# Scaling and masking half of the attention scores on ScalarE instead of VectorE, in the steps of a perceiver layer that have no value product

## The reference

```python
B, L, D = 32, 64, 128; S = 1601; HEADS, HEAD_DIM = 16, 64
q = layernorm(x) @ Wq                         # 32 x 64 tokens, 16 heads
k = ctx @ Wk; v = ctx @ Wv                    # 32 x 1601 keys, 16 heads
q = rms_norm(q, q_norm_w); k = rms_norm(k, k_norm_w)
scores = einsum('bhld,bhsd->bhls', q, k) / sqrt(64)
scores = where(mask, scores, -1e9)            # mask[b, s] = s < length[b], the same for all heads
attn = softmax(scores); o = einsum('bhls,bhsd->bhld', attn, v)
x = x + o.reshape(b, l, 1024) @ Wo
```

## Time and profile before

| what | value |
|---|---|
| median of 3 runs | 2440.9 us (2440.45 to 2441.34) |
| the profiled execution | 2441.62 us, its span 2439.8 us |
| TensorE busy | 2328.2 us, 95% of the span |
| VectorE busy | 2096.5 us, 86% |
| ScalarE busy | 1360.0 us, 56% |
| GpSimd busy | 1489.3 us, 61% |
| granted TensorE clock, mean | 0.988 |

### The profile page before, as it was taken

The page is one execution under the profiler, slowest core; times in us unless marked ns, Lnnn a source line. Parts: engine busy times, 40 slices in busy tenths (PEclk is TensorE's granted clock), DMA queues, the critical chain, the costliest instruction groups (busy, mean ns, idle before and its releaser), DMA issues. The chain is left out here.

```text
span 2439.8 us, 57496 instructions
## 1 busy us (share of the span) xinstructions
PE 2328.2 (95%) x16407; PEld 1937.4 (79%) x16407; DVE 2096.5 (86%) x3358; ACT 1360.0 (56%) x2587; POOL 1489.3 (61%) x1069
## 2 busy tenths in 40 slices
PE   6888999999999999999999999999999999899975
PEld 3666888888888888888888888888888888766543
DVE  6779999999999999999999999999999997467666
ACT  4754555555555555555555555555555554255536
POOL 3446777777777777777777777777777761011100
PEclk9999999999999999999999999999999999999997
DMA  2432122222222222222222222222222215320000
GB/s 86 162 123 48 46 57 54 53 53 54 53 54 54 53 53 53 53 54 59 54 54 53 53 53 53 53 53 60 55 54 53 53 47 156 123 88 20 2 1 17
DMA packets 441100, 145.06 MB, mean 59 GB/s; under 512 B 365344, under 2 KB 423616, under 8 KB 440896
## 3 DMA queue, kind: packets, MB, share of 16 engines
q1 hardware_dynamic: 440880, 143.50, 23.7%
q10 hardware_dynamic: 144, 0.52, 0.1%
HBM read 109.17 MB, written 34.73 MB: 59 GB/s over the span
## 5 line engine op out<-in xcount | busy, mean ns | idle before, releaser
L456 POOL TENSOR_TENSOR probs<-arena,best_all 128x1024 f32 (+2 forms) x397 | 943.5, 2377 | 420.3 <-DVE best L835 396.5
L1079 PEld LDWEIGHTS u_ps<-rows,probs 128*128 128x128 f32 x6656 | 799.4, 191 | 59.5 <-issue 19.1
L1079 PE MATMUL u_ps<-rows,probs 128*128 (+1 forms) x6656 | 811.7, 275 | 10.6 <-ACT probs L661 5.0
L820 DVE SCALAR_TENSOR_TENSOR arena<-s_ps,mask,rrms 128x512 f32 (+2 forms) x832 | 603.9, 727 | 113.5 <-PE s_ps L956 111.4
L661 ACT ACTIVATE probs<-probs 128x1024 f32<-128x1024 f32 (+1 forms) x416 | 440.9, 1061 | 420.9 <-POOL probs L456 407.5
L795 DVE TENSOR_REDUCE ssq<-squares 128x16 f32<-128x1024 f32 (+2 forms) x416 | 490.5, 1179 | 40.2 <-ACT squares L619 39.2
L619 ACT ACTIVATE squares<-k_ps 128x512 f32<-128x512 f32 (+1 forms) x832 | 451.3, 591 | 41.4 <-PE k_ps L956 21.9
L835 DVE TENSOR_TENSOR best<-best,arena 128x1024 f32<-128x1024 f32 (+1 forms) x352 | 447.2, 1270 | 0.1
L954 PE MATMUL k_ps<-w_hi,cT_hi 128*128 128x512 f32 (+1 forms) x832 | 362.4, 436 | 4.5 <-ACT squares L619 4.4
L954 PE MATMUL s_ps<-q_hi,cT_hi 128*128 (+2 forms) x832 | 330.3, 397 | 3.0 <-DVE arena L820 3.0
L613 ACT ACTIVATE cT_hi<-cT 128x128 fp32r<-128x128 f32 (+1 forms) x416 | 129.2, 311 | 363.5 <-DVE cT L786 363.4
(11 more groups left out here) (233 smaller groups left out, 2155.6 us busy)
## 6 DMA issues: line engine op xcount, KB each, us to landing
stage<-in_ctx SPq DMA_DIRECT2D x1536, 16.0 KB, 1.7
rows<-in_ctx SPq DMA_DIRECT2D x32, 768.0 KB
queries<-probs SPq DMA_DIRECT2D x16, 1024.0 KB, 4.1
q_plain<-queries SPq DMA_DIRECT2D x32, 512.0 KB, 3.3
best_all<-best_rows SPq DMA_DIRECT2D x31, 512.0 KB, 3.9
u_transposed<-uT_sb SPq DMA_DIRECT2D x124, 128.0 KB, 2.6
a_uT<-u_transposed SPq DMA_DIRECT2D x10, 1024.0 KB, 4.9
arena<-u_transposed SPq DMA_DIRECT2D x6, 1024.0 KB, 5.0
```

The source lines that it names most:

```text
L456: pool.tensor_tensor(probs[0:r, slot_of(c, PRING), :], scores_at(b, c), best_all[0:r, bass.ds((b % 2) * HL, HL)], ALU.subtract).then_inc(s ...
L820: dve.scalar_tensor_tensor(out=scores_at(p, c, h * HALF, HALF).rearrange("p (h l) -> p h l", l=L), in0=s_ps[h][0:r, :].rearrange("p (h l) ...
L1079: last = pe.matmul(u_ps[g // 3][:, at:at + UW], probs[0:r, s, g * P:(g + 1) * P], rows, start=(c == 0 and g % 3 == 0), stop=(c == NC - 1), ...
```

## The change

In steps 0 to 19 ScalarE scales and masks the second bank, with eight instructions of one head (64 columns) each: rrms x score + mask, both factors pointer operands with one value for each partition. They stand behind `split_hi`. VectorE no longer does the second `scale` in these steps; behind its sum of squares it waits for ScalarE's count and then raises the semaphore `scaled` itself, which TensorE and `keep_best` wait for.

```diff
+        scaled_beside = sem("scaled_beside")
...
+            def scale_beside(p, n, c):
+                r = rows_of(c)
+                if n == 0:
+                    act.wait_ge(q_carried, 2 * TILES)
+                    act.wait_ge(mask_steps, 4)
+                act.wait_ge(rrms_ready.sem, rrms_ready.ended(p, 6 if c >= EARLY else 3))
+                act.wait_ge(scored.sem, scored.ended(n, 2))
+                for h in range(H // 2, H):
+                    last = act.activation(scores_at(p, c, h * L, L), s_ps[1][0:r, h * L - HALF:(h + 1) * L - HALF], ACT.Identity,
+                                          bias=mask[0:r, p * NC + c:p * NC + c + 1], scale=rrms[0:r, c * H + h:c * H + h + 1])
+                last.then_inc(scaled_beside, 1)
...
                 if on.turn:
                     split_hi(n + TURN_AHEAD, at_step(p, c, TURN_AHEAD)[1])
+                if on.scores and no_values(p, c):
+                    scale_beside(p, n, c)
...
-                if on.scores:
+                if on.scores and not no_values(p, c):
                     scale(p, n, c, 1)
                 if on.keys:
                     sum_squares(n + KEYS_AHEAD, at_step(p, c, KEYS_AHEAD)[1], no_values(p, c))
+                if on.scores and no_values(p, c):
+                    dve.wait_ge(scaled_beside, n + 1)
+                    dve.sem_inc(scaled.sem, 1)
```

## The result

The changed kernel takes 2470.0 us (median of 4 runs, 2467.71 to 2476.28) against 2440.68 (4 runs, 2437.15 to 2441.34): ratio 1.0129, 95% interval 1.0116 to 1.0142. That is 29.3 us slower; 2472 was forecast. The profiled execution is the longest of the four, 2476.28 us with a span of 2474.5, which is 6.3 us above the median.

A forecast was written before the change was run, and what follows sets the result against it. VectorE, nearly full at 3.24 us per step, bounds steps 0 to 19. A two-engine chain adds 33.8 us, Ln and Exp waits 1.2, swallowed stalls -4.6: +30.4, 2441.62 to 2472; range 2461 to 2481.

The forecast's parts named there:

- The ring: Steps 0 to 19: VectorE and ScalarE take turns, each waiting for the other; 4.93 us per step against 3.24.
- the eight: ScalarE's eight added instructions per step: 0.29 us from start to start, 0.40 for the last, 2.43 in all.
- hand-over and increment: From the end of ScalarE's eight instructions to VectorE's keep_best: 0.04 us plus 0.10 for VectorE's increment, together 0.14.
- plain step: One of steps 0 to 19 without one-off work, keep_best to keep_best: 3.24 us before, forecast 4.93.
- stretch: Steps 0 to 19, without value product, from first scale to step 20: 73.48 us before, forecast 104.
- Ln and Exp behind the eight: ScalarE's Ln and Exp, about 0.6 us, before VectorE's Newton instructions: three times, one covered by a block maximum; +1.2 us.
- The stalls that are swallowed: Longer steps absorb VectorE's waits and collisions in steps 0 to 19, all but one collision of 1.1 us: -4.6 us.
- The stretch after it unchanged: Everything from step 20 on, 1852.5 us with TensorE busy 1843.6, was to keep its length.
- The clock's rival: TensorE's idle time lowers its clock in steps 0 to 19: about 5 us more, 2477; chance 0.13 shared with dearer instructions.
- The faster side: Rival: VectorE loses 0.63 us of work per step without waiting; about 5 us gained, 2437; faster or no change 0.05.
- the squares' loop: ScalarE squares, GpSimd folds, VectorE sums through one buffer: 3.20 us per step, hidden by VectorE's 3.24.

The follow-up runs named there:

- e_order: Changed kernel with ScalarE doing its eight instructions ahead of the copy cT_hi instead of behind it: 2446.96 us, ratio 1.0028 to the kernel before.
- e_wide: Changed kernel with one ScalarE instruction of 512 columns, using one head's rms factor, instead of eight of 64: 2441.52 us, ratio 1.0011 to the kernel before.
- e_nobias: Changed kernel with the mask left out of the eight instructions (one pointer operand, Copy instead of Identity): 2456.27 us, ratio 1.0063 to the kernel before.
- e_sixteen: Changed kernel with sixteen ScalarE instructions of 32 columns instead of eight of 64: 2512.2 us, ratio 1.0295 to the kernel before.
- e_share: Changed kernel with ScalarE taking three heads ahead of cT_hi and VectorE the other five behind its transpose: 2440.79 us, ratio 1.0002 to the kernel before.
- e_filler: Changed kernel with six unneeded TensorE matmuls in each of steps 2 to 19, between the score banks: 2471.61 us, ratio 1.0132 to the kernel before.

## Why the prediction was right

The ring was there, for the reason given: `e_order` opens it, and `e_wide`, `e_nobias` and `e_sixteen` change its length. It was forecast with four terms; here they are by the timelines above.

| term | forecast | measured |
|---|---|---|
| keep_best to the end of the transpose | 2.14 | 2.14 |
| cT_hi to the next instruction | 0.22 | 0.22 |
| the eight | 2.43 | 2.46 |
| hand-over and increment | 0.14 | 0.20 |
| plain step | 4.93 | 5.02 |
| stretch | 104 | 104.58 |
| median of the runs | 2472 | 2470.0 |

- *The price of the eight* held. The group of the new instructions:

```profile
L631 ACT ACTIVATE arena<-s_ps,mask,rrms 128x64 f32<-128x64 f32 x152 | 46.7, 411 | 0.0
```

  0.411 for one, and (2.46 - 0.41)/7 = 0.293 from start to start, against 0.40 and 0.29 taken from other forms. By the figures of the Trainium skill, page "ScalarE: Activation LUTs", section "What ACT_TABLE_LOAD costs", it would have been, as an estimate, 0.425, 0.332 and 2.75 in all. They are too high here by 0.3 us for the eight, most of it in how much neighbours overlap (0.118 measured, 0.093 there). By them the forecast would have been 2478, again an estimate.
- *Hand-over* was 0.06 too small: from the end of the eight to keep_best it is 0.20. If the hand-over is 0.04 of it, as the prediction took it, VectorE's wait and increment take 0.16 and not 0.10; the split was not measured. With the 0.03 of the eight that is 20 x 0.09 = 1.8 us too little.
- *Ln and Exp behind the eight* were put at 0.6 for each of two. From keep_best to keep_best step 3 takes 6.02, 1.00 more than a plain one, of which 0.70 are Newton: 0.3. The Ln starts at 164.18, and the last of the eight ends at 164.33. Step 11, with its wider rows, takes 6.23, of which 0.86 are Newton: 0.35. Both together 0.7 instead of 1.2.
- *The stalls that are swallowed* came out as said at step 19 (keep_best 1.23 instead of 2.75) and a little better at step 14, where the collision left 1.82 instead of 2.29. The three small errors nearly cancel: 30.4 + 1.8 - 0.5 - 0.5 = 31.2, against 31.1 for the stretch. That they cancel is luck, and so in part is how near the median came: the forecast was worked out for the profiled execution, which came out at 2476.28, 4.3 above it, 3.6 of them outside the stretch, while the median came out 2.0 below.
- *"The stretch after it unchanged"* was wrong for the profiled execution. From keep_best to keep_best the step behind the 20 took 7.76 us instead of 4.45:

```profile
250.62 0.40 PE L974 MATMUL s_ps<-q_hi,cT_lo 128*128 128x512 f32 x1
251.93 3.78 PE L1097 MATMUL u_ps<-rows,probs 128*128 128x129 f32 x16 [0.91 <-issue]
255.36 0.78 PE L972 MATMUL k_ps<-w_hi,cT_hi 128*128 128x512 f32 x1
255.93 0.63 PE L973 MATMUL k_ps<-w_lo,cT_hi 128*128 128x512 f32 x1
```

  Sixteen value matmuls in 3.78 us and the next ones 0.63 long are TensorE at the lower of its clock levels (0.50 in the second window above), after it had idled 1.96 us and then 0.91. About half of the 3.3 us came back later, since from there to the last block transpose only 1.65 were added. Nor is this the change's alone: in `e_share`, with a granted clock of 0.98 over its stretch and the same idle 2.20 before the first value product as the kernel before, that step took 6.09 us, and the sixteen matmuls 3.67 against 2.02 in the kernel before (granted clock 0.60 from 217.71 to 222.00, and 1.00 from 220.87 to 225.31 in the kernel before).

```profile
217.90 3.67 PE L1107 MATMUL u_ps<-rows,probs 128*128 128x129 f32 x16 [2.20 <-issue]
```

- *The clock's rival* was right that the clock would fall, to 0.89 in the stretch, and wrong in what it would cost: in the step whose rows are mostly 0.63 long TensorE still ends ahead of the increment and idles 0.41 us, and `e_filler` has the same step at a clock of 1.00.

```profile
177.59 0.63 PE L972 MATMUL k_ps<-w_hi,cT_hi 128*128 128x512 f32 x1
180.49 0.50 PE L972 MATMUL s_ps<-q_hi,cT_hi 128*128 128x512 f32 x1 [0.41 <-DVEq L925]
```

- *The faster side*: `e_share` shows why there was next to nothing to win. With VectorE relieved, the squares' loop of 3.20 us is next.

## What to carry to other kernels

Moving work from a full engine to an idle one pays only if it doesn't close a chain through both. Follow the moved instruction on its new queue: what stands ahead of it and for whom that waits, and what on the old engine's queue stands behind the wait for it; if the two meet in one step, the step becomes the sum of both sides, and neither engine looks full (56% and 72% here). Then compare with the next loop that the full engine hid: here it was 0.04 us shorter, so even a placing that opens the ring gave nothing that could be told. And an instruction that handled eight heads with a broadcast operand is not replaced one for one by instructions that take one factor each: 0.63 us became 2.46.

## What the runs showed of the hardware

- A ScalarE row doesn't tell its price in a series. At 32 columns it is as long as at 64 (mean 0.411 in both); from start to start it is (4.39 - 0.41)/15 = 0.265 instead of 0.293.

```profile
L632 ACT ACTIVATE arena<-s_ps,mask,rrms 128x32 f32<-128x32 f32 x304 | 83.5, 411 | 0.5 <-PE s_ps L975 0.5
```

- A second pointer operand costs 0.085 us for each instruction (0.411 against 0.326, by the rows of the changed kernel and of the one without the mask, whose function is also Copy and not Identity).

```profile
L631 ACT ACTIVATE arena<-s_ps,rrms 128x64 f32<-128x64 f32 x152 | 32.9, 326 | 0.0
```

- Granted clock and time can part: 0.89 or 1.00 over the same 104.5 us, since TensorE was not in the chain.
